# Adding a bias to x by an accumulating DMA instead of a GpSimd addition, and scaling that bias on ScalarE instead of VectorE

## What is computed

```python
x = x + jnp.tanh(g_xattn[0]) * _L0_xattn_ref(_layernorm(x), ctx_4096, ...)      # product "a": round(LN(x)) @ round(ctx)
x = x + jnp.tanh(g_ffn[0]) * _L0_ffn_ref(_layernorm(x), L0_ffn_W_int, L0_ffn_scale_i32, L0_ffn_bias)   # product "b"
x = x + jnp.tanh(g_xattn[1]) * _L1_xattn_ref(_layernorm(x), ctx_4096, ctx_4096, Wq, Wk, Wv, Wo)
x = x + jnp.tanh(g_ffn[1]) * _L1_ffn_ref(_layernorm(x), weight_packed, scales)

def _L0_ffn_ref(x, W_int, scale_i32, bias):
    ...
    x_q = _quant_act_per_token(x, A_BITS)      # scale = max|row| / 127, round, clip
    return jnp.einsum('bsi,oi->bso', x_q, W) + bias
```

## Time and profile before

| | |
|---|---|
| median of 3 runs | 863.67 us (857.62 to 865.52) |
| the profiled execution | 859.74 us |
| its span in the trace | 857.9 us |
| PE busy | 826.9 us, 96% of the span |
| DVE busy | 589.9 us, 69% |
| POOL busy | 535.6 us, 62% |
| ACT busy | 448.3 us, 52% |

### The profile page before, as it was taken

One profiled execution on the slowest core, in us unless ns is written; L12 is line 12 of the kernel. 1 busy time (PEld: TensorE's weight loads), 2 busy tenths in 40 slices (PEclk: granted clock), 3 DMA queues, 4 the chain that ended last, 5 costly groups with the idle time before them and its releaser, 6 DMA issues.

```text
span 857.9 us, 14034 instructions
## 1 busy us (share of the span) xinstructions
PE 826.9 (96%) x4498; PEld 333.9 (39%) x4498; DVE 589.9 (69%) x850; ACT 448.3 (52%) x741; POOL 535.6 (62%) x235
## 2 busy tenths in 40 slices
PE   8799899899999999999999999999999989999998
PEld 7467644344444432222222222222222213444443
DVE  6886848988488557888888888888888500455622
ACT  4445445555322147777777777777777772111200
POOL 6455329966442417888889888888988886211200
PEclk9989999999999989999999999999999999999999
DMA  7999943336995213554464455456454334122341
GB/s 251 308 241 265 210 150 106 97 86 117 238 228 167 92 59 84 106 127 108 109 133 104 107 103 126 95 125 132 101 113 99 81 68 99 23 52 49 60 137 73
DMA packets 120822, 107.81 MB, mean 126 GB/s; under 512 B 85324, under 2 KB 105804, under 8 KB 116684
## 3 DMA queue, kind: packets, MB, share of 16 engines
q1 hardware_dynamic: 115120, 71.59, 32.1%
q0 software_dynamic: 4608, 33.56, 19.4%
q10 hardware_dynamic: 1052, 2.10, 0.8%
HBM read 41.55 MB, written 12.58 MB: 63 GB/s over the span
## 4 chain that ended last, share of the span: by engine, by line
PE 65%; POOL 10%; issue 7%; DMA 7%; POOLq 3%; DVE 3%; ACT 2%; DVEq 1%; ACTq 0%
PE sbank L1670 10%; PE sbank L1661 9%; PE mpair L1601 9%; POOL wraw L599 6%; DMA tail<-wraw 5%; POOLq L493 3%; PE sbank L1471 3%; PE sbank L1472 3%; PE sbank L1473 3%; PE sbank L1737 3%; PE sbank L1741 3%; PE sbank L1752 3%; PE sbank L1754 3%; PE sbank L1739 3%; POOL xT_lo L494 2%
## 5 line engine op out<-in xcount | busy, mean ns | idle before, releaser
L1333 DVE TENSOR_REDUCE mx<-mpair 128x1 f32<-128x1024 f32 x256 | 302.2, 1216 | 64.2 <-PE mpair L1601 63.2
L891 ACT ACTIVATE regC<-sbank 128x512 f32<-128x512 f32 x512 | 278.1, 594 | 107.6 <-PE sbank L1661 105.6
L1661 PE MATMUL sbank<-regD 98*128 98x512 f16 x512 | 179.5, 386 | 7.9 <-ACT regC L891 5.6
L599 POOL TENSOR_TENSOR wraw<-regC 128x2048 f32<-128x2048 f32 x32 | 148.9, 4652 | 28.6 <-DMA tail<-wraw 17.6
L1601 PE MATMUL mpair<-regD 96*128 96x512 f16 x512 | 157.3, 383 | 0.9 <-DVE mx L1333 0.3
L1670 PE MATMUL sbank<-regC,regD 128*32 128x512 f32 x1024 | 137.2, 608 | 1.0 <-ACT regC L891 1.0
L1661 PEld LDWEIGHTS sbank<-regD 98*128 98x128 f16 x512 | 48.7, 97 | 187.2 <-ACT regC L891 145.9
L599 POOL TENSOR_TENSOR regD<-regC 128x2048 f32<-128x2048 f32 x16 | 75.6, 4727 | 19.5 <-ACT regC L891 19.5
L599 POOL TENSOR_TENSOR tail<-regC 128x2048 f32<-128x2048 f32 x16 | 76.8, 4801 | 0.2 <-ACT regC L891 0.2
L1601 PEld LDWEIGHTS mpair<-regD 96*128 96x128 f16 x512 | 48.0, 98 | 55.1 <-DVE mx L1333 13.8
L492 POOL TENSOR_SCALAR xT_lo<-xT_lo,sc 128x1024 f32<-128x1024 f32 x16 | 30.1, 1878 | 43.7 <-DVE X L1001 35.4
(11 more groups left out here) (185 smaller groups left out, 1255.4 us busy)
## 6 DMA issues: line engine op xcount, KB each, us to landing
regD<-wraw POOLq DMA_DIRECT2D x16, 1024.0 KB, 7.0
tail<-wraw POOLq DMA_DIRECT2D x16, 1024.0 KB, 6.9
xT_lo<-in_ctx SPq DMA_DIRECT2D x16, 512.0 KB, 4.7
wraw<-in_L_ffn_W_int SPq DMA_DIRECT2D x8, 512.0 KB, 4.7
X<-in_x SPq DMA_DIRECT2D x4, 1024.0 KB, 7.2
wraw<-in_L_xattn_Wq SPq DMA_DIRECT2D x8, 512.0 KB, 3.7
wraw<-in_L_xattn_Wo SPq DMA_DIRECT2D x8, 512.0 KB, 4.3
regD<-q_hi_scratch SPq DMA_DIRECT2D x32, 128.0 KB, 2.4
```

Source lines behind the costliest of these rows:

```text
L599: nc.gpsimd.tensor_tensor(p_sum[pr if pr < 3 else 1][:, :, :], probs[:, (2 * pr) % 4, :, :], probs[:, (2 * pr) % 4 + 1, :, :], ALU.add).th ...
L891: nc.scalar.activation(probs[:, kt % 4, h, :], bank[4 + h % 2], ACT.Exp, scale=SCALE).then_inc(s["exp_ok"], 1)
L1333: v.tensor_reduce(mx[m][:, bass.ds(n, 1)] if par is not None else mx[m][:, n:n + 1], slot[:, :, :], AX.XY, ALU.max).then_inc(s["mx_red"], 1)
L1661: pe.matmul(bank[4 + h % 2], kst[par][0:98, kt * P:(kt + 1) * P], qst[par][0:98, h * 512:(h + 1) * 512], start=True, stop=True).then_inc(s ...
```

## The change

The scaled bias is still added to each tile of x at the same place of POOL's list, but as a DMA that POOL issues and that adds `biasB` into `X[:, t]` in SBUF. Its landing is counted on two semaphores, `bias_add0` for even tiles and `bias_add1` for odd ones, 16 counts for each DMA, and from tile 2 on POOL first waits for the DMA of two tiles before. DVE's `b_out(t)` waits for the landing of its tile. The scaling of the bias by TF0 leaves DVE's list and stands in ACT's, behind `ln2_round(1)`.

```diff
             def add_bias(t):
                 pool.wait_ge(s["ln2_dev"], t + 1)
-                nc.gpsimd.tensor_tensor(X[:, t, :], X[:, t, :], biasB, ALU.add).then_inc(s["bias_add"], 1)
+                if t >= 2:
+                    pool.wait_ge(bias_add[t % 2], 16 * (t // 2))
+                pool.sem_inc(s["pool_gate"], 1)
+                nc.gpsimd.dma_start(X[:, t, :], biasB, accum_op=ALU.add).then_inc(bias_add[t % 2], 16)
...
+            def bias_scale():
+                act.wait_ge(s["bias_in"], 16)
+                nc.scalar.activation(biasB, biasB, ACT.Copy, scale=TF0).then_inc(s["bias_ok"], 1)
+
             ln2_deviation(0)
             wq_high(0)
             for t in range(T):
                 ln2_round(t)
+                if t == 1:
+                    bias_scale()
...
-            def bias_scale():
-                dve.wait_ge(s["bias_in"], 16)
-                v.tensor_scalar(biasB, biasB, TF0, None, ALU.mult).then_inc(s["bias_ok"], 1)
-                d()
-
             def ab_out(i):
                 kind, t = AB_OPS[i]
                 if kind == "a":
                     dve.wait_ge(s["x_c2"], t + 1)
                 else:
-                    dve.wait_ge(s["bias_add"], t + 1)
+                    dve.wait_ge(bias_add[t % 2], 16 * (t // 2 + 1))
...
                 a_stats(t)
-                if t == 2:
-                    bias_scale()
             ln2_scales(0)
```

More of the change, by code:

```diff
@@ L189, in build @@
             ab_mm ab_ev
-            ln2_stat ln2_dev ln2_inv ln2_q ln2_ready ln2_sd xt2_ev0 xt2_ev1 bias_add
+            ln2_stat ln2_dev ln2_inv ln2_q ln2_ready ln2_sd xt2_ev0 xt2_ev1 bias_add0 bias_add1
             ln3_stat ln3_sd ln3_aff y3_ok y3_hi y3_lo xt3a_hi xt3a_lo xt3b_hi xt3b_lo xt3c_hi xt3c_lo
@@ L208, in build @@
         xt2_ev = [s["xt2_ev0"], s["xt2_ev1"]]
+        bias_add = [s["bias_add0"], s["bias_add1"]]
         xt3_hi = [s["xt3a_hi"], s["xt3b_hi"], s["xt3c_hi"]]
```

## The result

| | before | after |
|---|---|---|
| median of 22 runs each | 861.73 us (857.62 to 865.52) | 864.85 us (861.18 to 881.71) |
| the profiled execution | 859.74 us | 863.76 us |
| its span | 857.9 us | 861.9 us |
| PE busy | 826.9 us | 822.0 us |
| DVE busy | 589.9 us | 586.4 us |

The ratio after to before is 1.0039, with a 95% interval of 1.0026 to 1.0052: about 3.4 us slower, where 5.2 us faster were forecast. Executions more than 1.5% above the quickest of the same kernel are in the medians and not in the ratios: here three of the 22, at 876.4, 880.3 and 881.7 us. DVE and POOL are less busy, PE has the same matmuls, and ACT has one instruction more of 1.13 us; new besides are eight DMAs of 512 KB. So the loss is not more work for an engine: something waits.

What follows compares the result with a forecast made beforehand. PE was taken as the bound, losing 5.41 us to a wait for DVE and low clock; 5.4 less 0.2 for new waits, DMAs costing 0, gave 5.2 off 863.67: 858.5 us, range 853 to 865.

Steps and rivals of the forecast that it cites:

- the costing of the DMAs on POOL: On POOL: 0.57 us waiting plus 0.87 issuing per DMA against 2.36 for the addition; nothing for the end.
- The landing: Each 512 KB accumulating DMA lands in 4.5 us, bounds 3.7 and 8.5; cost 0 to 1.0 us, taken as 0.
- Rival C: At SP's query stores: last DMA holds xt3 transposes, store 5.4 us late, 7.1 lost, 865.6 us; chance 0.05.
- The main term: Before a6 on PE: 3.73 us wait plus 1.68 at low clock, 5.41 us, all of it to go.
- Both holds by L521: POOL's bias additions delay DVE's ln2_clip(2) by 2.0 us and L1225 by 1.9; with DMAs both delays go.
- `ln2_reduce(2)` waits for ACT: On DVE: the scaling moved to ACT delays ln2_deviation(2), a wait of about 1 us; 1.5 of 2.5 us remain.
- rival B: DVE's long steps wait for their own operands, not POOL; only the scaling's 1.5 us comes, 862.2 us; chance 0.05.
- Rival A: POOL's other two-input instructions hold DVE afresh; gain 4.1 down to 0.4 us, time middle 861.5; chance 0.18.
- 158.85: Forecast start in us of DVE's b_out(0), 4.4 us earlier than 163.25, so a6's wait goes with 0.7 to spare.

Runs made afterwards that it cites:

- the DMAs alone: Against the kernel before: bias added by accumulating DMAs as in the change, its scaling left on DVE; ratio 1.0056, median 866.34 us.
- scaling back on DVE: Against the changed kernel with semaphore for the drain and tile 7's bias by instruction: bias scaled on DVE again; ratio 0.996, median 857.44 us.
- the probe: Kernel before plus three plain 512 KB DMAs of the scaled bias to unused DRAM, ahead of wq_low(3), (4) and (5); one execution, 862.36 us.

## Why the prediction was wrong

It forecast 5.2 us gained, and 3.4 were lost. By the ratios the 8.6 us between them are some 2.8 for the drains (1.0039 to 1.0006), 2.7 for the last DMA (1.0006 to 0.9975) and 3.1 between the 5.2 forecast and the 2.1 that are gained once both are away; by the intervals each of these can be off by about 2 us. That the median of 864.85 is still inside 853 to 865, by 0.15 us, is luck: the forecast started from 863.67, the median of three runs, and 22 give 861.73.

- **The step that failed** is the costing of the DMAs on POOL: "POOL pays 0.57 of waiting for its own last instruction and 0.87 of issuing for each [...]: nothing for the end". The issue does cost 0.87. But the step names only what POOL pays at the DMA, and not what is queued behind it: the drain inside `wq_low`, which became a wait of 5 us four times. The runs put its price at 6.8 us for the kernel with seven DMAs, and at 2.8 for the one with eight, which without them waits 3.19 instead of 1.67 us for the held transpose. The prediction does not mention that drain at all, so its cost was put at nothing without a reason.
- **The landing** was taken as 4.5 us between bounds of 3.7 and 8.5. It is 6.7 in the median, 4.5 for the quickest. As a wait on the way to `b_out` this made no difference, as the prediction had worked out; through the drain it sets how long each gap is. That the size is the same as that of the plain load was no good reason to take the value near it: the 1024 KB accumulating DMA of the earlier trace rows, with 6.9, was nearer.
- **Rival C** had the right mechanism, an accumulating DMA among the `xt3` transposes that holds SP's queue, with 3.9 us more for the transpose (measured 3.3 more). It was given 0.05, on the grounds that the DMA is a quarter of the load's size and that the transposes would start earlier. Half a megabyte is enough, and the transposes started 3.2 us later. Its price is 1.7 to 3.2 us of waiting and not 7.1, since it meets the first transposed tile and not the store.
- **The main term**, 5.41 us for the wait before a6 with its low clock, was read from one execution. The kernel without any bias gains 3.9 us, within 1.9 to 5.8. In the control (the kernel before with a semaphore) that wait is 2.64 us and a6 takes 3.61, at full clock:

```profile
165.27 3.61 PE L1583 MATMUL mpair<-regR,xT_hi 128*128 128x512 f16 x16 [2.64 <-DVE X L1197]
```

So the low clock behind it is not there in every execution. Some 4 us would have been the better value, but the runs don't rule 5.4 out.
- **What held.** Both holds by L521 went, and a6 has no low clock; ACT's scaling takes 1.13 us; `ln2_reduce(2)` waits for ACT, 0.67 us; nothing on DVE waits for a landing. The reading of the earlier trace rows, that DVE was held by POOL's two-input instructions, stands, and rival B falls. (Its 0.17 us at 177.10 is an instruction of two elements in a row; the one of four also takes 0.17 in the changed kernel, at 157.05.)
- **Rival A and some luck.** Such a meeting did come, on the clip at 139.13, ahead of the whole change. By the start of `ln2_reduce(1)` (141.44 against 139.19) it and the later start of the block put DVE back by 2.25 us, nearly all of the 2.58 by which `b_out(0)` missed 158.85. That a6 waited only 0.20 us even so is luck: PE was 1.7 us late as well. In the second trace of the changed kernel it waits 1.50.

The rule of "SBUF — State Buffer" in the Trainium skill, in the box on the trap of DMAs from GpSimd in its section on the two sides of SBUF, is that GpSimd can't write descriptors while DVE has the port pair; it was cited against the change. The eight issues take 0.86 to 1.17 us, so beside the 0.87 of the earlier trace rows none was held for more than 0.3 us: no run here shows the rule at work, and it had no part in the loss.

## What to carry to other kernels

Before an instruction is replaced by a DMA from the same engine, read that engine's list on to its next drain: on GpSimd each drain seen here waited until the DMA had landed. Where it is there for the instruction ahead of it, a semaphore on that instruction does the same, at no cost that can be measured (0.9997). And count what else is in the DMA queues in the microseconds in which the new transfer is in flight, transposes above all: leave out the one transfer that meets them, and take the rest. And look at what the first trace has by chance: a short clip here was short in one trace of fourteen.

## What the runs showed of the hardware

- **GpSimd's drain and its DMAs**: 3.3 to 6.1 us of gap with an accumulating DMA of 512 KB right ahead (the change, the DMAs alone, drains with tile 7 by instruction), 1.4 to 1.9 with a plain one, 0.14 to 0.23 with none in flight. The gap ends 0.1 to 0.3 us after the landing.
- **An accumulating DMA lands late**: 512 KB in 6.7 us, hardly less than the 6.9 of 1024 KB; a plain one of 512 KB from the same engine in 3.1. The plain one went to DRAM and the other within SBUF, so accumulation is not the only difference.
- **It holds transposes of another queue**: 4.5 to 4.7 us instead of 1.3 for the second transpose that SP begins after it, in all four traces in which tile 7's bias goes by DMA (the change twice, with the semaphore, the DMAs alone). And one begun 0.8 us after it landed in 6.0 us instead of 3.1 (the DMAs alone; scaling back on DVE).
- **The low clock after a wait**: PE's granted clock fell to 0.50, that is 1.2 GHz, after waits of 5.50 (the change), 3.98 to 4.05 (three traces), 3.73 (before), 3.31 (the probe), 3.18 (the DMAs alone), 3.06 (scaling back on DVE) and even 2.30 us (the DMAs alone, at the query projection: 1.00 in 219 to 221 us, 0.50 in 221 to 223). It stayed at 1.00 after 3.19 (with the semaphore) and 2.64 us (the control). The length of the wait alone doesn't tell it. Nor does the first matmul behind it: after the wait of 4.05 us four took 0.38 us, and then they took 0.64.
- **Who holds whom changes with little**: DVE's instructions of 0.2 to 0.5 us took 1.0 to 3.0 beside POOL's two-input ones, and which of them did so differed from kernel to kernel and between two traces of the changed one (the first clip 2.39 and 1.44 us).
